# Splitting two more key chunks and sharing every low half with GpSimd

## The chip, the cores and the metric

The kernel runs on one core of one Trainium2 chip. The metric is the device time of one launch in microseconds; a change is measured against the kernel before on the same chip.

## The reference

Cross attention of 128 queries over 12,544 context rows, then a linear attention and a gated feed-forward on the 128 rows. The change touches only the scores of the cross attention (`Sim`, whose rows go through a softmax):

```python
Sim = (encoder_hc @ w1)[:, :, None] + (decoder_hq @ w2)[:, None, :] \
    + jnp.einsum('bid,bjd->bij', encoder_hc * w3, decoder_hq) + b_sim[0]
A = jax.nn.softmax(Sim, axis=2)
hq_hat = jnp.einsum('bij,bjd->bid', A, decoder_hq)
...
x = x + _L0_xattn_ref(_layernorm(x, axis=-1), ctx_1024, ...)
x = x + _L0_attn_ref(_layernorm(x, axis=-1), ...)
x = x + _L0_ffn_ref(_layernorm(x, axis=-1), ...)
```

## The kernel before, in words

The context is read twice from HBM: first transposed, as 25 key chunks of 512 columns (the last has 256), then as 25 chunks of rows. Each chunk is 512 KB and lands in one of ten slots of `raw`. SyncE issues all the loads in order (L396 to L413); a load into a slot waits (`wait_for_slot`, L380) until the slot's old content has been used: for a native chunk its matmuls, for a split chunk VectorE's low half, for a shared chunk GpSimd's part as well.

In the **key stage** TensorE computes `scores(k)` for k = 0 to 24 (L912). A **native** chunk (`NATIVE`, L35) multiplies fp32 keys from `raw` by the fp32 queries (L925). A **split** chunk is first taken apart into `pair`: ScalarE copies the keys rounded to the matmul format fp32r (the high half, `keys_high`, L488), VectorE subtracts that from the keys (the low half, `keys_low`, L698). TensorE then makes three passes over it, each of two matmuls: queries high by keys high (L940), queries low by keys high (L944), queries high by keys low (L954). `pair` has five buffers, used in turn. For a **shared** chunk (`SHARED`, L36) VectorE makes only the first 576 of the 1024 columns of the low half, and GpSimd the last 448 (L449 to L456). GpSimd's part of chunk k waits for VectorE's low half of the split chunk before k and for ScalarE's high half of k; TensorE waits for it only before the last matmul of the third pass (L953).

VectorE's queue in this stage is written out by hand (L758 to L762): for each pair of chunks (2e, 2e+1) the low halves of chunks 2e+2 and 2e+3 (none for native ones), then `running_max(e)` (L721), which takes the scores of chunks 2e and 2e+1 out of PSUM, negates them and carries the running maximum on. TensorE may be six chunks ahead of it (L919). ScalarE's queue (L557 to L579) holds the high halves in order, with work on the weights between them behind chunks 8, 12, 13, 16, 17, 18, 20 and 22.

In the **row stage** the scores become probabilities (ScalarE, L507), TensorE turns them (L968), ScalarE and VectorE split the turned block (L520, L728), and TensorE multiplies it by the rows (L997, L999). The rows are split too: ScalarE copies the first 512 columns of the high half (L488), GpSimd casts the other 512 (L463), VectorE makes the low half of all 1024 (L698). `row_use(k)` counts the split chunks through both stages, so the number of split key chunks moves the buffers that the row stage uses. The first two row chunks are multiplied in fp32 (L979). A short **tail** behind it does the rest of the layer.

Of the kernel before, what the change touches and what calls it, by code (L numbers as in the profile page):

```python
# [31 lines left out]
LATE = CHUNKS - 2  # L32
EARLY = 2
EPS = 1e-5
NATIVE = (0, 4, 8, 16, 24)  # L35
SHARED = (10, 12, 14, 18, 20, 22)  # L36
POOL_COLUMNS = 448
W_BEHIND = (12, 18)

# [22 lines left out]
def build(nc, x, keys_in, keys_last_in, rows_in, rows_last_in, weights_in, vec_in, bias_in, const_in, out):  # L62
# [6 lines left out]
    def width_of(k):  # L69
        return tiles_of(k) * P  # L70

    def is_native(k):

        return k in NATIVE

# [24 lines left out]
    with ExitStack() as stack:  # L100
# [271 lines left out]
        def keys_part(buf, k, a):  # L372
            return buf[:, a * width_of(k):(a + 1) * width_of(k)]
# [5 lines left out]
        def _(sp):  # L379
            def wait_for_slot(item):  # L380
# [10 lines left out]
                else:  # L391
                    sp.wait_ge(low_done, split_before[before] + 1)
                    if before in SHARED:
                        sp.wait_ge(pool_low_done, SHARED.index(before) + 1)

# [23 lines left out]
        def _(pool):  # L419
# [16 lines left out]
            for a in range(DH):  # L436
# [11 lines left out]
                                    ALU.mult, ALU.add).then_inc(mu_left_done, 1)  # L448
            for n, k in enumerate(SHARED):  # L449
                use = split_before[k]  # L450
# [236 lines left out]
        def _(dve):  # L687
# [8 lines left out]
            def take_low(item, use, columns):  # L696
                dve.wait_ge(high_done, use + 1)
                nc.vector.tensor_tensor(out=pair[:, use % PAIR_BUFS, 1, 0:columns], in0=raw[:, slot(item), 0:columns],  # L698
                                        in1=pair[:, use % PAIR_BUFS, 0, 0:columns].bitcast(F32), op=ALU.subtract)\
                    .then_inc(low_done, 1)  # L700

            def keys_low(k):

                take_low(k, split_before[k], ITEM - POOL_COLUMNS if k in SHARED else width_of(k) * DH)

# [200 lines left out]
        def _(pe):  # L906
# [5 lines left out]
            def scores(k):  # L912
# [36 lines left out]
                for a in range(DH):  # L949
                    if use == 0 and a > 0:  # L950
                        pe.wait_ge(low_done, 1)
                    if k in SHARED and a == DH - 1:
                        pe.wait_ge(pool_low_done, SHARED.index(k) + 1)  # L953
                    last = nc.tensor.matmul(out_ps, q_high[:, a, :], keys_part(low, k, a), start=False,  # L954
# [273 lines left out]
```

## Time and profile before

| | us |
|---|---|
| median of 3 runs (lowest to highest) | 112.36 (111.89 to 112.43) |
| the profiled execution | 112.1 |
| its span, first to last instruction | 110.3 |
| TensorE busy | 105.1 (95%) |
| VectorE busy | 93.1 (84%) |
| ScalarE busy | 82.4 (75%) |
| GpSimd busy | 29.3 (27%) |

Times within the trace are counted from the start of the span. The granted TensorE clock was 1.0 over the whole span. PE is TensorE's matmuls and PEld its weight loads, DVE is VectorE, ACT ScalarE, POOL GpSimd, SPq the queue of SyncE. The recorded length of an instruction overlaps the next one by some 0.1 us on VectorE and more on TensorE, so that paces are read from start to start.

### The profile page before, as it was taken

How to read it: one execution, taken by the hardware profiler on the slowest of the kernel's cores; microseconds unless marked ns; L12 is line 12 of the kernel's file. 1: busy time of each engine (PE TensorE's matmuls, PEld its weight loads, DVE VectorE, ACT ScalarE, POOL GpSimd, SP SyncE). 2: the span in 40 equal slices, each digit the busy share in tenths (PEclk: the TensorE clock that was granted, in tenths of full speed). 3: DMA queues.
4: the chain of work that ended last, by engine and by line, in shares of the span. 5: the costliest groups of instructions: out<-in, count | busy, mean ns of one | idle time of the engine just before them, and what ended most of it. 6: DMA issues, size and time to landing. Idle time of an engine off the chain costs nothing.

```text
span 110.3 us, 1855 instructions
## 1 busy us (share of the span) xinstructions
PE 105.1 (95%) x582; PEld 86.4 (78%) x583; DVE 93.1 (84%) x152; ACT 82.4 (75%) x171; POOL 29.3 (27%) x47
## 2 busy tenths in 40 slices
PE   5999999999999999999999999999999998998890
PEld 2368768588858888899899999989898997887680
DVE  1478999999998998999999999999999847674352
ACT  5067668899979989999999899988976725903450
POOL 2239200444043314233242424286330000200100
PEclk9999999999999999999999999999999999999999
DMA  2999999999999999999999999960000000000001
GB/s 72 367 406 423 416 422 422 416 422 422 409 420 417 418 415 423 417 420 442 442 389 423 415 422 425 406 260 0 3 0 0 0 6 0 0 0 0 6 3 48
DMA packets 8220, 29.82 MB, mean 270 GB/s; under 512 B 1042, under 2 KB 1298, under 8 KB 8082
## 3 DMA queue, kind: packets, MB, share of 16 engines
q1 hardware_dynamic: 8064, 29.69, 66.3%
q8 instruction: 5, 0.08, 0.3%
q14 instruction: 5, 0.04, 0.1%
q10 hardware_dynamic: 146, 0.01, 0.1%
HBM read 29.57 MB, written 0.13 MB: 269 GB/s over the span
## 4 chain that ended last, share of the span: by engine, by line
PE 94%; DVE 1%; issue 1%; ACT 1%; DVEq 0%; ACTq 0%
PE mixed_ps L997 18%; PE scores_ps L968 10%; PE mixed_ps L999 9%; PE scores_ps L940 8%; PE scores_ps L944 8%; PE scores_ps L954 8%; PE scores_ps L925 7%; PE scores_ps L910 4%; PE scores_ps L979 3%; PE scores_ps L1090 2%; PE mixed_ps L1142 2%; PE side_ps L1016 1%; PE scores_ps L1155 1%; PE side_ps L1133 1%; PE scores_ps L1016 1%; PE scores_ps L1125 1%
## 5 line engine op out<-in xcount | busy, mean ns | idle before, releaser
L698 DVE TENSOR_TENSOR pair<-raw,pair 128x1024 fp32r<-128x1024 f32 (+2 forms) x42 | 49.0, 1183 | 1.3 <-ACT pair L488 1.0
L488 ACT ACTIVATE pair<-raw 128x512 fp32r<-128x512 f32 (+1 forms) x42 | 34.5, 820 | 3.8 <-DMA raw<-keys_dram 3.4
L997 PE MATMUL mixed_ps<-pair,turned_high 128*128 128x512 f32 x84 | 32.3, 418 | 0.0
L999 PE MATMUL mixed_ps<-pair,turned_low 128*128 128x256 f32 x84 | 23.6, 281 | 0.0
L463 POOL CAST pair<-raw 128x512 fp32r<-128x512 f32 x22 | 13.6, 619 | 27.3 <-DVE pair L698 23.1
L997 PEld LDWEIGHTS mixed_ps<-pair,turned_high 128*128 128x128 f32 x84 | 15.8, 188 | 2.8
L520 ACT ACTIVATE turned_high<-scores_ps 128x512 fp32r<-128x512 f32 (+1 forms) x23 | 13.4, 584 | 4.0 <-PE scores_ps L968 4.0
L721 DVE TENSOR_SCALAR_CACHE_REDUCE neg_scores<-scores_ps,neg_max 128x1024 f32<-128x1024 f32 (+1 forms) x13 | 15.8, 1216 | 0.2
L999 PEld LDWEIGHTS mixed_ps<-pair,turned_low 128*128 128x128 f32 x84 | 16.0, 190 | 0.0
L728 DVE TENSOR_TENSOR turned_low<-scores_ps,turned_high 128x512 fp32r<-128x512 f32 (+1 forms) x23 | 15.3, 667 | 0.2 <-ACT turned_high L520 0.2
L968 PE MATMUL scores_ps<-ident,neg_scores 128*128 128x128 f32 x98 | 14.6, 272 | 0.0
L940 PE MATMUL scores_ps<-pair,q_high 128*128 128x512 f32 x40 | 14.1, 434 | 0.0
L507 ACT ACTIVATE neg_scores<-neg_scores,neg_max 128x1024 f32<-128x1024 f32 (+2 forms) x14 | 13.7, 977 | 0.0
L968 PEld LDWEIGHTS scores_ps<-ident,neg_scores 128*128 128x128 f32 x98 | 11.7, 140 | 1.4
L944 PE MATMUL scores_ps<-pair,q_low 128*128 128x512 f32 x40 | 12.5, 393 | 0.0
L954 PE MATMUL scores_ps<-pair,q_high 128*128 128x512 f32 x40 | 12.4, 391 | 0.0
L454 POOL TENSOR_TENSOR pair<-raw,pair 128x448 fp32r<-128x448 f32 x6 | 6.9, 1154 | 20.5 <-DVE pair L698 20.5
L940 PEld LDWEIGHTS scores_ps<-pair,q_high 128*128 128x128 f32 x40 | 7.5, 188 | 3.1 <-issue 1.9
L954 PEld LDWEIGHTS scores_ps<-pair,q_high 128*128 128x128 f32 x40 | 7.5, 188 | 1.7
L944 PEld LDWEIGHTS scores_ps<-pair,q_low 128*128 128x128 f32 x40 | 7.5, 188 | 1.6
L925 PE MATMUL scores_ps<-raw,q_t 128*128 128x512 f32 (+1 forms) x20 | 8.6, 553 | 0.0
L430 POOL TENSOR_TENSOR ln_rstd<-ln_var,minus_half 128x1 f32<-128x1 f32 x3 | 1.7, 555 | 21.8 <-DVE ln_var L842 12.7
(189 smaller groups left out, 130.6 us busy)
## 6 DMA issues: line engine op xcount, KB each, us to landing
raw<-keys_dram SPq DMA_DIRECT2D x24, 512.0 KB, 10.0
raw<-rows_dram SPq DMA_DIRECT2D x24, 512.0 KB, 9.2
w<-weights_dram SPq DMA_DIRECT2D x1, 1792.0 KB, 9.9
w<-weights_dram SPq DMA_DIRECT2D x2, 512.0 KB, 10.4
const<-const_dram SPq DMA_DIRECT2D x1, 832.0 KB, 11.5
raw<-keys_last_dram SPq DMA_DIRECT2D x1, 256.0 KB, 10.2
raw<-rows_last_dram SPq DMA_DIRECT2D x1, 256.0 KB, 6.8
x_sb<-x_dram SPq DMA_DIRECT2D x1, 128.0 KB, 2.2
```

The source lines that it names most:

```text
L488: nc.scalar.activation(pair[:, use % PAIR_BUFS, 0, 0:columns], raw[:, slot(item), 0:columns], ACT.Copy)\
L507: nc.scalar.activation(neg_scores[:, first:last], neg_scores[:, first:last], ACT.Exp, bias=neg_max[:, EVICTIONS:EVICTIONS + 1], scale=-1.0 ...
L698: nc.vector.tensor_tensor(out=pair[:, use % PAIR_BUFS, 1, 0:columns], in0=raw[:, slot(item), 0:columns], in1=pair[:, use % PAIR_BUFS, 0, 0 ...
L721: nc.vector.tensor_scalar(neg_scores[:, first_col:last_col], scores_ps[:, first // 2 % 3, scores_at:scores_at + last_col - first_col], -1. ...
L728: nc.vector.tensor_tensor(out=turned_low[:, k % TURNED_BUFS, 0:width_of(k)], in0=probs_turned_ps[k % TURNED_BUFS][:, 0:width_of(k)], in1=t ...
L925: last = nc.tensor.matmul(out_ps, q_t[:, a, :], keys_part(raw[:, slot(k), :], k, a), start=(a == 0), stop=(a == DH - 1))
L940: nc.tensor.matmul(out_ps, q_high[:, a, :], keys_part(high, k, a), start=(a == 0), stop=False)
L944: nc.tensor.matmul(out_ps, q_low[:, a, :], keys_part(high, k, a), start=False, stop=False)
L954: last = nc.tensor.matmul(out_ps, q_high[:, a, :], keys_part(low, k, a), start=False, stop=(a == DH - 1))
L968: last = nc.tensor.transpose(probs_turned_ps[k % TURNED_BUFS][:, t * P:(t + 1) * P], neg_scores[:, col:col + P], ident[:, :])
L997: nc.tensor.matmul(mixed_ps[:, :].rearrange("p (h d) -> p h d", h=2), probs_high, both[:, :, t * D:(t + 1) * D], start=(k == EARLY and t = ...
L999: last = nc.tensor.matmul(mixed_ps[:, 0:D], probs_low, rows_tile(high, t), start=False, stop=(k == LATE - 1 and end))
```

## The change

Two constants. Chunks 8 and 16 are no longer native; the shared chunks are all from 6 to 23 instead of six even ones.

```diff
-NATIVE = (0, 4, 8, 16, 24)
-SHARED = (10, 12, 14, 18, 20, 22)
+NATIVE = (0, 4, 24)
+SHARED = tuple(range(6, 24))
 POOL_COLUMNS = 448
```

So `scores(8)` and `scores(16)` take the split branch, ScalarE and VectorE get `keys_high` and `keys_low` of both, VectorE's low halves of chunks 6 to 23 have 576 columns, and GpSimd's loop over `SHARED` has 18 parts of 448 columns, each with its wait for the low half of the chunk before (`low_done`), in SyncE's `wait_for_slot`, and in TensorE's third pass.

## Rows read from the trace of the kernel before

**Rows 1.** The page: busy time of the engines, the chain that ended last, key loads.

```profile
PE 105.1 (95%) x582; PEld 86.4 (78%) x583; DVE 93.1 (84%) x152; ACT 82.4 (75%) x171; POOL 29.3 (27%) x47
...
PE 94%; DVE 1%; issue 1%; ACT 1%; DVEq 0%; ACTq 0%
...
raw<-keys_dram SPq DMA_DIRECT2D x24, 512.0 KB, 10.0
```

**Rows 2.** The chain in order of time: start us, length us, what.

```profile
19.22 1.72 PE scores_ps L925 x4
20.93 0.45 PE scores_ps L940 x2
21.39 0.46 PE scores_ps L944 x2
21.85 0.46 PE scores_ps L954 x2
...
30.54 1.72 PE scores_ps L925 x4
...
35.92 0.46 PE scores_ps L954 x2
...
40.05 0.47 PE scores_ps L954 x2
...
41.89 0.44 PE scores_ps L968 x4
42.33 0.87 PE scores_ps L925 x4
```

**Rows 3.** Busy time by engine from 22.77 to 25.78 us: PE, PEld, DVE, ACT, POOL.

```profile
22.77:25.78 3.01, 3.01 (x14) 2.46 (x14) 3.01 (x6) 2.80 (x6) 1.16 (x1) 1.00 1.02 416
```

**Rows 4.** Timeline of VectorE, key stage: start us, length us (of all merged), instruction.

```profile
13.94 1.28 DVE L721 TENSOR_SCALAR_CACHE_REDUCE neg_scores<-scores_ps,neg_max 128x1024 f32<-128x1024 f32 x1
...
22.77 1.28 DVE L721 TENSOR_SCALAR_CACHE_REDUCE neg_scores<-scores_ps,neg_max 128x1024 f32<-128x1024 f32 x1
23.97 1.89 DVE L698 TENSOR_TENSOR pair<-raw,pair 128x576 fp32r<-128x576 f32 x2
24.64 1.22 DVE L698 TENSOR_TENSOR pair<-raw,pair 128x1024 fp32r<-128x1024 f32 x1
25.78 1.28 DVE L721 TENSOR_SCALAR_CACHE_REDUCE neg_scores<-scores_ps,neg_max 128x1024 f32<-128x1024 f32 x1
...
38.92 1.88 DVE L698 TENSOR_TENSOR pair<-raw,pair 128x576 fp32r<-128x576 f32 x2
```

**Rows 5.** Timeline of GpSimd, the same stretch.

```profile
22.93 1.16 POOL L454 TENSOR_TENSOR pair<-raw,pair 128x448 fp32r<-128x448 f32 x1 [1.86 <-DVE pair L698]
```

**Rows 6.** Timelines of VectorE and GpSimd, 8.8 to 11.6 us.

```profile
9.18 2.36 DVE L698 TENSOR_TENSOR pair<-raw,pair 128x1024 fp32r<-128x1024 f32 x2 [0.50 <-ACT pair L488]
...
8.80 0.19 POOL L440 TENSOR_TENSOR b_kept<-b_c 128x2 f32<-128x2 f32 x1
8.95 0.20 POOL L442 TENSOR_TENSOR b_mean_sum<-b_mean 128x1 f32<-128x1 f32 x1
9.22 1.22 POOL L445 TENSOR_TENSOR mean_const<-b_mean_sum,ln_mv 128x1 f32<-128x1 f32 x1
10.41 1.18 POOL L447 TENSOR_SCALAR mu_left<-vec 128x4 f32<-128x4 f32 x1
```

**Rows 7.** The same at 44 to 46 us, and lengths of L698 (ns, min/median/max).

```profile
44.23 0.62 POOL L463 CAST pair<-raw 128x512 fp32r<-128x512 f32 x1 [0.62 <-DMA raw<-rows_dram]
...
44.24 2.81 DVE L698 TENSOR_TENSOR pair<-raw,pair 128x1024 fp32r<-128x1024 f32 x2
...
45.84 1.21 DVE L698 TENSOR_TENSOR pair<-raw,pair 128x1024 fp32r<-128x1024 f32 x1
...
L698 DVE TENSOR_TENSOR pair<-raw,pair x42: 675/1220/1681, 9.2 to 85.5; 128x1024 fp32r<-128x1024 f32 x35, 128x576 fp32r<-128x576 f32 x6, 128x512 fp32r<-128x512 f32 x1
```

**Rows 8.** The same in the row stage, one chunk.

```profile
66.37 0.62 POOL L463 CAST pair<-raw 128x512 fp32r<-128x512 f32 x1 [1.23 <-DVE pair L698]
...
66.73 1.32 DVE L698 TENSOR_TENSOR pair<-raw,pair 128x1024 fp32r<-128x1024 f32 x1
67.98 0.68 DVE L728 TENSOR_TENSOR turned_low<-scores_ps,turned_high 128x512 fp32r<-128x512 f32 x1
```

**Rows 9.** ScalarE: high halves, busy time from 26 to 32 us, who waited.

```profile
15.33 0.51 ACT L547 ACTIVATE x_c<-x_sb,x_neg_mean 128x256 f32<-128x256 f32 x1
16.70 1.06 ACT L488 ACTIVATE pair<-raw 128x1024 fp32r<-128x1024 f32 x1 [0.86 <-DMA raw<-keys_dram]
...
26.00:32.00 6.00, 6.00 (x25) 4.32 (x23) 6.00 (x8) 5.38 (x13) 1.81 (x2) 1.00 1.02 414
...
33.55 1.22 DVE L698 TENSOR_TENSOR pair<-raw,pair 128x1024 fp32r<-128x1024 f32 x1 [0.47 <-ACT pair L488]
```

## The prediction

> **What bounds the kernel now.** I read the page first. TensorE is busy for 95% of the span and is 94% of the chain that ended last [rows 1], so the first question for any edit is what it does to TensorE's queue. The chain in order of time [rows 2] gives the queue's true pace, without the overlap that the mean durations hold: a native key chunk (fp32 straight from raw) takes 1.72 us (chunk 8 at 19.22, chunk 16 at 30.54), a split chunk three passes of 0.46 us, 1.37 in all, and each piece begins where the one ahead ends. There is no gap in it from chunk 4 to the row stage, and behind the keys the chain goes on unbroken (probabilities turned at 41.89, the short chunk 24 at 42.33). So in the key stage TensorE is the bound, at 2.75 us for a pair of split chunks.
>
> Next come the engines that feed it, because a faster TensorE is worth only what they can follow. VectorE was busy in all of the 3.01 us of the pair from 22.77 to 25.78, and ScalarE in 2.80 of them [rows 3]. From start to start VectorE's pieces are [rows 4]: the maximum over a pair of chunks (L721) 1.20 us (22.77 to 23.97), a low half of 576 columns 0.67 (23.97 to 24.64), one of all 1024 columns 1.14 (24.64 to 25.78). That is 3.01 for a pair of which one chunk is shared with GpSimd, slower than TensorE's 2.75; VectorE lives off a lead that it won before, and by the end little is left. It starts low half 22 at 38.92 and ends it at 39.59, and TensorE's third pass over it starts at 40.05 [rows 2, 4]. So the key stage is close to having VectorE as its bound.
>
> GpSimd's part of a shared chunk (L454, 448 columns) takes 1.16 us. In the kernel before it is released by VectorE's low half of the odd chunk ahead, so it starts together with the maximum: 22.93 to 24.09, beside L721 from 22.77 to 23.97 [rows 4, 5]. The two never run low halves side by side, but for 0.1 us. After the change they must.
>
> **What a low half and a GpSimd instruction do to each other.** This is the row that decides the case. Two tiny GpSimd instructions on 2 columns and 1 column took 0.19 and 0.20 us at 8.80 and 8.95, when VectorE stood idle. The next, on 1 column, started at 9.22, 0.04 us behind a low half of 1024 columns (9.18), and took 1.22 us: it ended at 10.44, when that low half was over (10.32). The one at 10.41 took 1.18 beside the second low half [rows 6]. So a running low half (two SBUF inputs) holds GpSimd off to its end, and GpSimd then gets its turn ahead of the next one. The other way round: at 44.23 a GpSimd cast of 0.62 us started together with a low half at 44.24, and VectorE's next low half came only at 45.84, 1.60 later and not 1.14; the slowest of all low halves is 1681 ns [rows 7]. The cast cost VectorE 0.46 us, its whole length but for the last 0.16. At 66.73 a low half met the last 0.26 us of a cast (66.37 to 66.99) and took 1.25 from start to start, 0.11 more than 1.14 [rows 8]: again all but the last 0.15. The maximum reads PSUM, and it took 1.28 with GpSimd beside it as it did without [rows 4]. My reading is mutual exclusion between low halves and GpSimd's reads.
>
> The Trainium skill speaks against this change too (SBUF — State Buffer, "Who interferes with whom"): a VectorE instruction with two SBUF inputs and a GpSimd instruction that reads SBUF exclude each other for the whole instruction, the second waiting until the first ends. The rows agree on the block, but show it 0.15 us shorter than the whole; taken to the letter, the rule would put 0.14 us more on each of the eight waits below, some 1 us on the sum.
>
> **The change, part by part.** (1) Chunks 8 and 16 split: TensorE saves 2 x (1.72 - 1.37) = 0.69 us, if it is fed. (2) ScalarE gets two high halves of 1.06 us [rows 9]. The first fits into the 0.86 us in which it waited for data at 15.84 and the slack behind; the second falls in 26 to 32, where ScalarE has 0.62 us idle, so that later high halves come about 0.4 us later. Alone this is hidden: low half 19 waited 0.47 us for ScalarE at 33.55 [rows 9], shrinks by 0.47, and TensorE has its third pass over it at 35.92. I cost it at nothing; the price if the cover is gone is the 0.4. (3) VectorE: 12 low halves of the 18 chunks go from 1.14 or nothing to 0.67: ten shrink by 0.47 (4.7 us saved), two are new (1.34 spent), 3.4 us less work. (4) GpSimd goes from 6 to 18 parts, 18 x 1.16 = 21 us of work in the 28 us of these chunks (13.94 to 41.89). (5) The load into a slot now waits for GpSimd's part as well; the queue is some 10 us of transfers deep (10.0 us from issue to landing [rows 1]), so a release some us late costs nothing in the key stage, and rows are read far later. (6) The buffer numbers of the row stage move by two; no cost.
>
> Without exclusion VectorE would need 1.20 + 2 x 0.67 = 2.54 us a pair, under TensorE's 2.75: that is the good case. With it the pair runs like this. GpSimd's part of an odd chunk is released by the low half of the even one, finds VectorE in the odd low half, and starts when that ends, which is when the maximum starts. It takes 1.16. The part of the next even chunk, long released, follows at once, at +1.16, while the maximum ends at +1.20: VectorE's even low half comes 0.04 us too late and waits until GpSimd's read ends, 1.16 - 0.14 after its start, at +2.18. Then two low halves, 1.34. The period is 1.20 + 0.98 + 1.34 = 3.52 us. Were VectorE first at that point, GpSimd's part would slip in between the two low halves and the period would be the same.
>
> Where it starts: low halves 6 and 7 run 15.14 to 16.48 (the maximum ahead of them starts at 13.94 [rows 4]). GpSimd's part 7 then runs 16.48 to 17.64, its part 8 from 17.64, and VectorE's low half 8, due at about 17.9, gets in at 18.66 and ends at 19.33. Seven periods on, low half 22 ends at 19.33 + 7 x 3.52 = 43.97, where it now ends at 39.59. TensorE's third pass over 22 starts some 0.13 later, at 44.10 instead of 40.05: 4.05 us late. GpSimd's part 23 runs 44.64 to 45.80, which adds 0.14 before the last matmul of chunk 23. The 0.69 is inside this sum, since TensorE now waits. The row stage behind is TensorE's own and moves as a whole. Sum: +4.2 us. The profiled execution took 112.1 (span 110.3), so it would be 116.3; the median of the runs is 112.36, 0.26 above it, and I forecast 116.5.
>
> Bounds on the one unknown, how long a 448-column tensor_tensor of GpSimd holds VectorE off, which no row shows for more than 0.16 us: the cast held it for 0.46 of 0.62, 74%; at that share a part would hold it 0.86 and not 1.02, the period is 3.36 and the sum 3.1. At 1.16 in full and 0.05 us between, the period is 3.7 and the sum 5.4. I take 1.02, since both casts show a fixed tail of about 0.15.
>
> **The rivals.** *No exclusion between these two instructions* (GpSimd's part reads two inputs by turns and may leave room). Place: VectorE's even low half. Price: none, and the gain of part (1) stands, 112.36 - 0.69 = 111.7. It decides from where VectorE's wait is below 2.75 - 2.54 = 0.21 us a pair. For it: at 22.93 and five more times such a part overlaps the low half by 0.1 us without harm. Against it: the tail of a cast does none either, and the body of one does; and low halves would in any case hold GpSimd off, as 9.22 shows.
> *Partial exclusion:* half the wait, 0.49 a pair. Low half 8 ends at 18.84, the period is 3.03, and low half 22 ends at 18.84 + 7 x 3.03 = 40.05; TensorE's third pass starts at 40.18 and not 40.05, and with the 0.14 of part 23 that is 0.3 us, 112.6.
> *ScalarE sets the pace* after the exclusion turns out harmless: the 0.4 us of part (2) eats most of the 0.69, giving about 112.1, within the measurement.
> *The change does nothing* is excluded: both constants enter the loops directly.
>
> **How the numbers follow.** Full exclusion, +3.1 to +5.4: 0.80. No exclusion with the gain: 0.11. Partial exclusion or a late ScalarE: 0.09, of which two thirds lie within 0.5% (0.56 us, about what a measurement of this kernel can tell from no change). So faster 0.11, same 0.06, slower 0.83. The range runs from 114.0, below the low bound of 115.5 since the hold may be softer than a cast's, to 118.0, the high bound; it leaves out the cases near 112.
>
> **What would show it.** In the profile after: low halves (L698) of 576 columns in two kinds, about 0.75 us and about 1.7, the long ones on even chunks; L454 of odd chunks at 1.6 to 1.7 us, as their wait is inside the record; maxima starting 3.5 us apart; TensorE idle before L954 for 0.8 us a pair; the turn at 41.89 moved to about 46. If instead all L698 stay at 0.75 and the maxima stand 2.75 apart, the exclusion was wrong and the time is 111.7. If the hold is real but the time moved little, look for a period near 3.0. If ScalarE is late, VectorE's idle time before L698 names L488.

## The result and the profile after

The changed kernel takes 115.88 us (median of 6 runs, 115.45 to 116.51); the kernel before, run beside it, 112.18 (111.89 to 112.43). The ratio is 1.0335, with a 95% interval from 1.03 to 1.037: slower by 3.7 us. The profiled execution took 116.03 us, its span is 114.3. Ratios leave out the launches in a slower state of the chip and medians do not, so that below a ratio can be a little smaller than the medians make it. Beside the experiments the kernel before had medians of 112.21 to 112.43.

From the page of the kernel after, the lines that answer to [rows 1], and what the DMA engines moved in 40 equal slices of the span:

```profile
PE 107.0 (94%) x586; PEld 85.8 (75%) x587; DVE 96.6 (85%) x154; ACT 84.3 (74%) x173; POOL 44.6 (39%) x59
...
GB/s 98 351 412 417 423 422 416 423 422 417 417 417 415 414 419 359 298 310 270 361 402 386 420 416 422 422 384 46 3 0 0 6 0 0 0 0 3 6 0 46
...
PE 57%; DVE 18%; issue 11%; DMA 7%; SPq 2%; ACT 2%; DVEq 0%; ACTq 0%
```

The busy shares hardly tell that anything happened: TensorE stands at 94% and was at 95%. The chain does. TensorE has fallen from 94% of it to 57%, and VectorE, which had 1%, has 18%, with 11% of "issue", time for which the profile names no cause. In order of time, two pairs of the key stage:

```profile
26.36 0.75 DVE pair L698
27.11 1.20 DVE neg_scores L721 x2
28.32 0.06 DVE pair L698
28.38 1.41 issue
29.79 0.74 DVE pair L698
30.53 1.21 DVE neg_scores L721 x2
...
43.60 0.73 PE scores_ps L954 x2
...
45.79 0.44 PE scores_ps L968 x4
```

The chain runs through VectorE with a period of 3.42 us: maximum 1.20, the even low half with what it waits (0.06 and 1.41 of "issue"), the odd one 0.74. It gets back to TensorE at 43.60, at the third pass over chunk 22, and the turn that was at 41.89 [rows 2] is at 45.79, 3.90 us later. The span grew by 4.0. So all of the loss but 0.1 us was made in the key stage.

The timeline of VectorE in that stretch, and that of GpSimd:

```profile
28.24 2.29 DVE L698 TENSOR_TENSOR pair<-raw,pair 128x576 fp32r<-128x576 f32 x2
30.45 1.27 DVE L721 TENSOR_SCALAR_CACHE_REDUCE neg_scores<-scores_ps,neg_max 128x1024 f32<-128x1024 f32 x1
31.66 0.08 DVE L721 DVE_READ_ACCUMULATOR neg_scores<-scores_ps,neg_max 128x1 f32 x1
31.66 2.29 DVE L698 TENSOR_TENSOR pair<-raw,pair 128x576 fp32r<-128x576 f32 x2
33.88 1.27 DVE L721 TENSOR_SCALAR_CACHE_REDUCE neg_scores<-scores_ps,neg_max 128x1024 f32<-128x1024 f32 x1
```

```profile
29.94 2.72 POOL L454 TENSOR_TENSOR pair<-raw,pair 128x448 fp32r<-128x448 f32 x2 [0.70 <-DVE pair L698]
33.36 2.73 POOL L454 TENSOR_TENSOR pair<-raw,pair 128x448 fp32r<-128x448 f32 x2 [0.70 <-DVE pair L698]
```

Two low halves of 576 columns take 2.21 us from start to start (28.24 to 30.45), where two unhindered ones take 2 x 0.67 = 1.34 [rows 4]: VectorE waits 0.87 us a pair. GpSimd's two parts follow each other without a gap, the first already waiting while VectorE makes the odd low half. One blocked low half by itself, the low halves of 576 columns as a group (us busy, mean ns) after and before, and GpSimd's parts (ns: min/median/max) show the blocked ones of both engines:

```profile
21.40 1.62 DVE L698 TENSOR_TENSOR pair<-raw,pair 128x576 fp32r<-128x576 f32 x1
...
L698 DVE TENSOR_TENSOR pair<-raw,pair 128x576 fp32r<-128x576 f32 x18 | 19.8, 1139 | 0.0
...
L698 DVE TENSOR_TENSOR pair<-raw,pair 128x576 fp32r<-128x576 f32 x6 | 4.5, 754 | 0.0
...
L454 POOL TENSOR_TENSOR pair<-raw,pair x18: 1143/1380/1617, 14.4 to 43.6; 128x448 fp32r<-128x448 f32 x18
```

The waits within these records are in no list of waits, since no semaphore ends them; VectorE's idle time before L698 is 1.1 us in all. What the list of waits does name is the victim:

```profile
PEld scores_ps L954 <- DVE pair L698: 5.1, 7, 0.7
...
PE scores_ps L954 <- DVE pair L698: 2.1, 7, 0.3
PEld scores_ps L954 <- POOL pair L454: 1.8, 8, 0.2
```

### The profile page after: what moved, and what is told of

Same layout as the page of the kernel before. It is cut to its first block, busy times and chain, and to the rows that moved or that the text cites. A ratio compares the mean times of both kernels' runs of the same rounds, so it can differ in the third digit from the quotient of the medians.

```text
span 114.3 us, 1905 instructions
## 1 busy us (share of the span) xinstructions
PE 107.0 (94%) x586; PEld 85.8 (75%) x587; DVE 96.6 (85%) x154; ACT 84.3 (74%) x173; POOL 44.6 (39%) x59
## 4 chain that ended last, share of the span: by engine, by line
PE 57%; DVE 18%; issue 11%; DMA 7%; SPq 2%; ACT 2%; DVEq 0%; ACTq 0%
PE mixed_ps L997 17%; DVE neg_scores L721 10%; PE scores_ps L968 9%; PE mixed_ps L999 9%; DVE pair L698 7%; DMA raw<-keys_dram 7%; PE scores_ps L979 3%; SPq L401 2%; PE scores_ps L1090 2%; PE mixed_ps L1142 1%; PE side_ps L1016 1%; PE scores_ps L954 1%; PE scores_ps L1155 1%; PE side_ps L1133 1%; PE scores_ps L1016 1%
## 5 line engine op out<-in xcount | busy, mean ns | idle before, releaser
L698 DVE TENSOR_TENSOR pair<-raw,pair 128x1024 fp32r<-128x1024 f32 (+2 forms) x44 | 52.5, 1213 | 1.1 <-ACT pair L488 1.1
L488 ACT ACTIVATE pair<-raw 128x512 fp32r<-128x512 f32 (+1 forms) x44 | 36.2, 830 | 2.8 <-DMA raw<-keys_dram 2.5
L454 POOL TENSOR_TENSOR pair<-raw,pair 128x448 fp32r<-128x448 f32 x18 | 24.6, 1380 | 11.3 <-DVE pair L698 11.3
L954 PE MATMUL scores_ps<-pair,q_high 128*128 128x512 f32 x44 | 15.0, 422 | 2.1 <-DVE pair L698 2.1
L940 PE MATMUL scores_ps<-pair,q_high 128*128 128x512 f32 x44 | 14.6, 412 | 0.0
L944 PE MATMUL scores_ps<-pair,q_low 128*128 128x512 f32 x44 | 13.7, 393 | 0.0
L954 PEld LDWEIGHTS scores_ps<-pair,q_high 128*128 128x128 f32 x44 | 7.7, 188 | 7.9 <-DVE pair L698 5.1
L940 PEld LDWEIGHTS scores_ps<-pair,q_high 128*128 128x128 f32 x44 | 8.2, 188 | 2.5 <-issue 0.7
L944 PEld LDWEIGHTS scores_ps<-pair,q_low 128*128 128x128 f32 x44 | 8.3, 188 | 1.9
L910 PE MATMUL scores_ps<-idle 128*128 128x512 bf16 x12 | 5.0, 568 | 1.2 <-DVE idle L733 1.2
## 6 DMA issues: line engine op xcount, KB each, us to landing
const<-const_dram SPq DMA_DIRECT2D x1, 832.0 KB, 11.6
```

What stands on the lines that cost most here:

```text
L454: nc.gpsimd.tensor_tensor(out=pair[:, use % PAIR_BUFS, 1, shared], in0=raw[:, slot(k), shared], in1=pair[:, use % PAIR_BUFS, 0, shared].bi ...
L488: nc.scalar.activation(pair[:, use % PAIR_BUFS, 0, 0:columns], raw[:, slot(item), 0:columns], ACT.Copy)\
L940: nc.tensor.matmul(out_ps, q_high[:, a, :], keys_part(high, k, a), start=(a == 0), stop=False)
L944: nc.tensor.matmul(out_ps, q_low[:, a, :], keys_part(high, k, a), start=False, stop=False)
```

## The experiments

Two theories stood against each other. **Exclusion:** a low half with two SBUF inputs and a GpSimd instruction that reads SBUF cannot run together; what two of GpSimd's parts stick out beyond the maximum, VectorE waits. **The chain of semaphores:** GpSimd is merely slow, or its waits and VectorE's are linked in a ring of 3.42 us, and no resource is shared. In the profiles the key stage is measured from the start of chunk 4 to the turn before chunk 24, since the first keys land some tenths earlier or later from one execution to the next, which moves everything behind them: 13.21 to 41.73 us in the timeline of the kernel before, 28.52 us; 13.05 to 45.63 after, 32.58, so +4.06.

### VectorE's second operand from PSUM

```diff
-in1=pair[:, use % PAIR_BUFS, 0, 0:columns].bitcast(F32)
+in1=side_ps[:, 0:1].to_broadcast([P, columns])    # the 576-column low halves only
```

> The changed kernel, but VectorE's 576-column low halves read their second operand from PSUM (one column, spread) and not from SBUF, so the low halves of the shared chunks are not the keys' own. The order of the work, the waits, the sizes and GpSimd's parts stay. Theory (a low half with two SBUF inputs and GpSimd's SBUF reads exclude each other): both exclusions go, L698 of 576 columns is 0.75 to 0.8 us throughout, L454 1.15 throughout, the maxima stand 2.75 us apart (TensorE's pace), and the time is 0.4 to 0.7 us below the kernel before, 111.5 to 111.8. Rival (the 3.42 us come from the chain of semaphores and from GpSimd's own length, or from any overlap with it): L454 and the maxima stay as after, about 115.9.

Measured: 112.53 us, ratio 1.0029 (0.9989 to 1.0069). Its groups, and a stretch of VectorE's timeline (the edit moved line 698 to 701, and 721 to 724):

```profile
L454 POOL TENSOR_TENSOR pair<-raw,pair 128x448 fp32r<-128x448 f32 x18 | 20.6, 1162 | 8.2 <-DVE pair L701 5.2 <-ACT pair L488 3.0
...
L701 DVE TENSOR_TENSOR pair<-raw,side_ps 128x576 fp32r<-128x576 f32 x18 | 12.9, 749 | 1.5 <-ACT pair L488 1.5
```

```profile
22.33 1.29 DVE L724 TENSOR_SCALAR_CACHE_REDUCE neg_scores<-scores_ps,neg_max 128x1024 f32<-128x1024 f32 x1
23.54 0.08 DVE L724 DVE_READ_ACCUMULATOR neg_scores<-scores_ps,neg_max 128x1 f32 x1
23.54 1.41 DVE L701 TENSOR_TENSOR pair<-raw,side_ps 128x576 fp32r<-128x576 f32 x2
25.08 1.28 DVE L724 TENSOR_SCALAR_CACHE_REDUCE neg_scores<-scores_ps,neg_max 128x1024 f32<-128x1024 f32 x1
```

The same queues, waits and columns, and only one operand of VectorE's low halves differs: it stands in PSUM, and it is one column spread over 576. All 18 parts of GpSimd are 1132 to 1175 ns, all 18 low halves near 749, and the maxima stand 2.75 us apart, TensorE's pace, but for two places where VectorE waited for a high half of ScalarE (0.38 us at 30.16, 1.10 at 33.88); no third pass of TensorE waited in the stage. The key stage is 27.82 us (13.54 to 41.36), 0.70 below the kernel before. The rival of the semaphore chain is out: it is the second SBUF input. (A single spread column in SBUF was not tried, so the place is not quite parted from the form; for the place speaks that GpSimd's part did not lengthen the maximum either, which reads PSUM: 1.27 to 1.28 us.) The median came out 0.7 to 1 us above what I expected, and cannot be told from the kernel before; the profiled execution (111.58) has the gain in its key stage and in its span, 109.8 against 110.3.

### GpSimd's part only writes

The `...` stand for what is left out, here and below; a semaphore, not shown, orders the two memsets.

```diff
-nc.gpsimd.tensor_tensor(out=pair[..., 1, shared], in0=raw[...], in1=pair[..., 0, shared], op=ALU.subtract)
+nc.gpsimd.memset(filler[:, :], 0.0)                              # 640 columns, unused
+nc.gpsimd.memset(pair[..., 1, shared].bitcast(F32), 0.0)         # 448 columns
```

> The changed kernel, GpSimd's part being two memsets that only write (640 columns of an unused tile, then its 448 columns of the low half, filled with zeros), so those columns are not the keys' own. Theory (it is GpSimd's reads that exclude a low half): the memsets take as long beside a low half as alone, L698 of 576 columns stays at 0.75, maxima 2.75 apart: 111.5 to 111.9. Rival (any access of GpSimd to SBUF excludes a low half): even low halves wait for the memsets, and time rises with them, over 113.

Measured: 112.62 us, ratio 1.0 (0.9959 to 1.0041). Its groups (L698 is L701 here):

```profile
L701 DVE TENSOR_TENSOR pair<-raw,pair 128x576 fp32r<-128x576 f32 x18 | 13.1, 755 | 2.7 <-ACT pair L491 2.7
L458 POOL MEMSET filler<- 128x640 f32 x18 | 11.4, 635 | 14.3 <-DVE pair L701 9.8 <-ACT pair L491 4.4
L459 POOL MEMSET pair<- 128x448 f32 x18 | 8.5, 474 | 0.0
```

GpSimd is busy for 1.11 us a part, nearly as long as before (1.15), and in its turn beside low halves with both inputs in SBUF: neither waits for the other. So the write side is free, and the exclusion is one of reads. Of the time I expected too much: it is that of the kernel before and not 0.5 to 0.9 less, and the maxima do not stand 2.75 us apart. Most stand 2.54 apart, the 1.20 + 2 x 0.67 that VectorE needs when nothing holds it off, and three stand 3.16 to 3.72 apart, since VectorE waited 2.7 us in three places of the stage for ScalarE's high halves. TensorE waited by it for a first pass (0.25 us, at 34.98) and for a third (0.45 us, at 37.56); the key stage is 28.65 us.

### GpSimd's part is a copy

```diff
-nc.gpsimd.tensor_tensor(out=pair[..., 1, shared], in0=raw[...], in1=pair[..., 0, shared], op=ALU.subtract)
+nc.gpsimd.tensor_copy(out=pair[..., 1, shared], in_=raw[...])
```

> The changed kernel, GpSimd's parts being copies of 448 columns (one SBUF input) and not differences (two), so that part of the low half is not the keys' own. Number of parts, waits and VectorE's work stay. Theory: the parts fall to 0.54 us (a cast of 512 takes 0.62), two of them fit beside a maximum, L698 of 576 stays at 0.75, maxima 2.75 apart: 0.3 to 0.7 below the kernel before, 111.5 to 111.9. Rival (the count of switches between the engines is what costs, not how long GpSimd reads): near after, 115 or more.

Measured: 112.23 us, ratio 0.9978 (0.9942 to 1.0014), above the 111.5 to 111.9 that I had given; the key stage 28.26 us, 0.26 below the kernel before. Its groups (L698 is L697 here):

```profile
L454 POOL CAST pair<-raw 128x448 fp32r<-128x448 f32 x18 | 14.3, 803 | 14.5 <-DVE pair L697 8.6 <-ACT pair L487 5.7
L697 DVE TENSOR_TENSOR pair<-raw,pair 128x576 fp32r<-128x576 f32 x18 | 13.1, 754 | 2.1 <-ACT pair L487 2.0
```

The low halves are 754 ns, so VectorE never waits for GpSimd; the copies are 803 ns on average (556 to 1084), as those that are released beside a low half wait for its end within their record. As many switches between the engines as after, but shorter reads, and the loss is gone. What is missing to the gain of 0.69 is again a third pass that waited once (0.46 us) behind a late ScalarE.

### How much GpSimd reads: 224 and 336 columns

```diff
-POOL_COLUMNS = 448
+POOL_COLUMNS = 224    # the other: 336
```

> The changed kernel with GpSimd's part cut from 448 to 224 columns in every chunk from 6 to 23, VectorE's low half 800 columns. Theory (VectorE waits for what GpSimd's reads stick out beyond the maximum): two parts of some 0.67 us, the first started at the end of the odd low half, are nearly over when the 1.20 us of the maximum are, so VectorE waits 0.15 us at most and a pair costs 1.20 + 2 x 0.90 = 3.0 to 3.15 us. Fewer columns on GpSimd are faster: 0.2 to 1.3 us over the kernel before, 112.4 to 113.5, against 115.9 with 448. Rival (what counts is how much work VectorE hands over): slower than after, above 116.

> The changed kernel with 336 columns for GpSimd. Theory (VectorE waits for what two parts stick out beyond the maximum of 1.20 us): a part is 0.91 us, the second one's reads end 1.60 us after the start of the maximum, VectorE waits 0.40 and a low half of 688 columns is 0.79: the period is 1.20 + 0.40 + 1.57 = 3.17 us, between 3.01 (224 columns) and 3.42 (448), and the time 113.8 to 114.6. Rival (a step and no slope, once GpSimd's parts no longer fit): near 3.4 and 115.5 or more.

Measured: 224 columns 113.08 us, ratio 1.0051 (1.0012 to 1.0089); 336 columns 114.15 us, ratio 1.0152 (1.0086 to 1.0218). VectorE's timelines, first 224, then 336:

```profile
23.18 1.28 DVE L721 TENSOR_SCALAR_CACHE_REDUCE neg_scores<-scores_ps,neg_max 128x1024 f32<-128x1024 f32 x1
24.38 0.09 DVE L721 DVE_READ_ACCUMULATOR neg_scores<-scores_ps,neg_max 128x1 f32 x1
24.38 1.89 DVE L698 TENSOR_TENSOR pair<-raw,pair 128x800 fp32r<-128x800 f32 x2
26.19 1.28 DVE L721 TENSOR_SCALAR_CACHE_REDUCE neg_scores<-scores_ps,neg_max 128x1024 f32<-128x1024 f32 x1
```

```profile
23.40 1.27 DVE L721 TENSOR_SCALAR_CACHE_REDUCE neg_scores<-scores_ps,neg_max 128x1024 f32<-128x1024 f32 x1
24.60 0.08 DVE L721 DVE_READ_ACCUMULATOR neg_scores<-scores_ps,neg_max 128x1 f32 x1
24.60 2.04 DVE L698 TENSOR_TENSOR pair<-raw,pair 128x688 fp32r<-128x688 f32 x2
26.57 1.27 DVE L721 TENSOR_SCALAR_CACHE_REDUCE neg_scores<-scores_ps,neg_max 128x1024 f32<-128x1024 f32 x1
```

The periods are 3.01, 3.17 (as worked out) and, with 448, 3.42 us. VectorE's own work falls with every column it hands over, from 3.0 to 2.54 us a pair, and the pair gets longer all the same: the wait grows from nothing over 0.4 to 0.87. Handing over less is faster, down to 224 columns; with none at all (the next run) it is slower again.

### No GpSimd at all

```diff
-SHARED = tuple(range(6, 24))
+SHARED = ()
```

> The changed kernel with no shared chunk: VectorE makes all low halves of 1024 columns alone. Theory: a pair costs VectorE 1.20 + 2 x 1.14 = 3.48 us against 3.42 with GpSimd, so sharing both chunks of a pair buys nearly nothing: maxima 3.48 apart, 4.0 to 4.6 us over the kernel before, 116.2 to 116.8. Rival (GpSimd's help is real, and the 3.42 has another cause that VectorE alone would have too): much slower than after, since VectorE then has 2 x 0.47 more a pair: a period near 4.3, over 120.

Measured: 117.4 us, ratio 1.0449 (1.0393 to 1.0505), somewhat over the range I gave. In its timeline of VectorE:

```profile
28.03 1.28 DVE L721 TENSOR_SCALAR_CACHE_REDUCE neg_scores<-scores_ps,neg_max 128x1024 f32<-128x1024 f32 x1
...
31.51 1.28 DVE L721 TENSOR_SCALAR_CACHE_REDUCE neg_scores<-scores_ps,neg_max 128x1024 f32<-128x1024 f32 x1
```

The period is 3.48 us, which is just 1.20 + 2 x 1.14. So from chunk 8 on the parts, 24.6 us of GpSimd's records in all, buy 0.06 us a pair: 0.94 saved on the low halves, 0.87 given back as waiting. The one pair that gains more is the first, low halves 6 and 7, where no second part holds VectorE off: 1.39 us (15.39 to 16.78 after) against 2.27 (15.34 to 17.61 here). The key stage is 33.56 us, 0.98 above after.

### The two halves of the change alone, and GpSimd beside the maximum only

Even parts, against the changed kernel:

```diff
-SHARED = tuple(range(6, 24))
+SHARED = tuple(range(6, 24, 2))
```

Sharing only, against the kernel before:

```diff
-SHARED = (10, 12, 14, 18, 20, 22)
+SHARED = tuple(k for k in range(6, 24) if k not in NATIVE)
```

> The changed kernel with GpSimd's parts on even chunks only (6, 8, ... 22), 448 columns each. Every part then runs beside a maximum. Theory: period 3.01 as in the kernel before, both L698 kinds unblocked (0.75 and 1.22), L454 1.15; VectorE falls 0.26 us a pair behind TensorE and the time is 0.1 to 0.5 us over the kernel before: 112.3 to 112.7. So the split of chunks 8 and 16 alone costs next to nothing, and the odd parts cost 3 us. Rival (the cost lies in the two split chunks): stays above 114.

> The kernel before with every split chunk from 6 to 23 shared, chunks 8 and 16 native: the other half of the change alone. Theory: period 3.42 where both chunks of a pair are split, but the pairs with chunks 8 and 16 have one low half less, and TensorE gives 0.34 us there: 0.4 to 1.2 us over the kernel before, 112.6 to 113.4, so the two halves of the change are not additive. Rival (sharing costs the whole 3.7 us by itself): 115 or more.

Measured: even parts 113.11 us, ratio 1.0062 (1.0023 to 1.01); sharing only 113.69 us, ratio 1.0113 (1.0029 to 1.0198). Both times are above the ranges I had given (112.3 to 112.7 and 112.6 to 113.4). Even parts have unblocked records of both engines (L698 of 576 columns 756 ns, L454 1163) and a period of 3.01; their key stage is 29.39 us, 0.87 longer than that of the kernel before. VectorE, 0.26 us a pair slower than TensorE, has used up its lead by 25.55, and from there on six third passes wait for it. From VectorE's timeline with sharing only:

```profile
28.62 1.27 DVE L721 TENSOR_SCALAR_CACHE_REDUCE neg_scores<-scores_ps,neg_max 128x1024 f32<-128x1024 f32 x1
...
30.49 1.27 DVE L721 TENSOR_SCALAR_CACHE_REDUCE neg_scores<-scores_ps,neg_max 128x1024 f32<-128x1024 f32 x1
...
33.65 0.76 DVE L698 TENSOR_TENSOR pair<-raw,pair 128x576 fp32r<-128x576 f32 x1 [1.20 <-ACT pair L488]
```

Sharing only has the period of 3.4 us where both chunks of a pair are shared, but the pairs with a native chunk are short (the maxima of 28.62 and 30.49 stand 1.87 us apart), and VectorE wins back a lead there twice. A fully shared pair puts it 0.67 us behind TensorE (3.42 against 2.75), a pair with a native chunk brings it 1.22 forward (1.87 against 1.72 + 1.37). The native chunks were that lead. Each half alone costs 0.87 and 1.34 us in the key stage; together they cost 4.06, since what the one uses up the other would have needed. Not all of the 1.34 is exclusion, though: the second lead was lost at 33.65, where VectorE waited 1.20 us for a high half of ScalarE, which had itself waited 1.12 us for a key load at 30.20. What that wait is worth is not separated.

### Two attempts at a faster kernel

Both are the kernel before with these constants, the first called split 8, the second odd 512:

```diff
-NATIVE = (0, 4, 8, 16, 24)
-SHARED = (10, 12, 14, 18, 20, 22)
+NATIVE = (0, 4, 16, 24)
+SHARED = (6, 8, 10, 12, 14, 18, 20, 22)
```

```diff
-NATIVE = (0, 4, 8, 16, 24)
-SHARED = (10, 12, 14, 18, 20, 22)
-POOL_COLUMNS = 448
+NATIVE = (0, 4, 16, 24)
+SHARED = tuple(range(7, 24, 2))
+POOL_COLUMNS = 512
```

> The kernel before with chunk 8 alone split and shared, and chunk 6 shared too, so that all parts are on even chunks and beside a maximum: (6, 8, 10, 12, 14, 18, 20, 22). Theory: TensorE saves 0.34 us on chunk 8; VectorE has 0.67 more for low half 8 and 0.47 less for 6, which its lead at that place takes; chunk 16 stays native and renews the lead. Expected 0.35 us below the kernel before at best, 111.8, within what can be told apart. Rival (the lead does not last, as in the kernel with even parts and both split): 112.5 to 113.

> The kernel before with chunk 8 split, chunk 16 native, and GpSimd's parts on the odd chunks (7, 9, ... 23) with 512 columns. A part of an odd chunk is released while VectorE makes the odd low half and begins exactly when the maximum does, so 512 columns (some 1.2 us) fit beside it. Theory: no low half waits for GpSimd, L454 is 1.6 to 1.7 us with its own wait, the period is 1.20 + 1.14 + 0.60 = 2.94 us against 3.01, and over eight pairs VectorE is 0.5 us less late than with chunk 8 split and even parts of 448: the time comes back to that of the kernel before, 112.0 to 112.6, or a little under. Rival (a part of 512 columns sticks out beyond the maximum): low half 10 and its followers wait and the time is above 113.

Measured: split 8 112.95 us, ratio 1.0055 (1.0022 to 1.0088); odd 512 113.25 us, ratio 1.0046 (1.0004 to 1.0088). The trace of the latter is of a launch of 590.95 us, and nothing is read from it; its time is above the 112.0 to 112.6 that I had given, and why stays open. Split 8 went the way of its rival: its waits show three third passes that came late by VectorE (0.38 us at 27.89, 0.45 at 36.79, 0.40 at 39.80), its maxima stand 3.01 apart where both chunks are split, and the key stage is 0.46 longer. Even one more split chunk is more than VectorE can follow. Of the versions with all the work in them none beat the kernel before.

## Why the prediction was right

**The bound and who follows it.** TensorE was the bound by a margin of some tenths over VectorE, as read from [rows 2, 4]. The gain of part (1), 0.69 us, is real: with VectorE's operand in PSUM the key stage is 0.70 us shorter. But that kernel does not compute the low halves, and no version that does had the gain.

**Exclusion.** Read from two tiny GpSimd instructions and two casts [rows 6 to 8], it held for the pair of instructions that no row had shown side by side: the place of one operand takes it away, writes do not cause it, and its price follows the columns.

**The period** was to be 1.20 + 0.98 + 1.34 = 3.52 us and is 3.42. The term that was off is the wait, 0.87 and not 0.98, and the step behind it is where the second part starts. I let the part of the odd chunk take its full 1.16 us, counted from the end of the low half that held it off. It takes some 0.1 less: in the trace the maximum starts at 20.20, with the end of the odd low half, and GpSimd's next part at 21.26:

```profile
21.26 1.14 POOL L454 TENSOR_TENSOR pair<-raw,pair 128x448 fp32r<-128x448 f32 x1
```

My reading is that a part that waits within its record has its beginning behind it when the low half ends; no row shows what it does in that time. The rest, reads that end some 0.14 us before the record does, was right: 21.26 + 1.14 - 0.14 = 22.26, and the low half of 0.67 that follows is over at 22.93. So the Trainium skill's rule (SBUF — State Buffer, "Who interferes with whom"), by which the block lasts for the whole instruction, would have given a wait longer still, by some 0.14 us; these traces do not bear that out to the letter. Its other sentence there, that a GpSimd instruction which only writes does not contend with two SBUF inputs, agrees with the memsets (755 ns for L698 beside them).

**The sum.** +4.2 us was forecast for the profiled execution: 4.05 at the third pass over chunk 22 and 0.14 for GpSimd's part 23. The pass began at 43.60 and not 44.10: seven periods of 3.42 give 0.7 less than seven of 3.52, and low half 8 ended at 19.53 and not 19.33, as VectorE's start lay 0.25 us later in this execution (the maximum of 13.94 in [rows 4] is at 14.19), low halves 6 and 7 took 0.05 more, and the first wait was 0.1 shorter too. That makes 3.55. The missing 0.27 lies in the pass itself, which has 0.73 us in the chain after and had 0.47. Most of that is my own mixing of two starts. The chain counts a pass that did not wait from the end of the pass ahead (40.05), and one that waited from its own first record. Matmul records overlap, and in TensorE's timeline the pass over chunk 22 started earlier, first before, then after:

```profile
39.88 0.63 PE L954 MATMUL scores_ps<-pair,q_high 128*128 128x512 f32 x2
...
43.60 0.73 PE L954 MATMUL scores_ps<-pair,q_high 128*128 128x512 f32 x2 [0.30 <-DVE pair L698]
```

So the pass was 3.72 us late, not 3.55, and having waited cost it 0.10 more. Part 23 cost 0.08 (L954 at 45.25, 0.54 us, in the chain). 3.72 + 0.10 + 0.08 = 3.90, where the turn is. That the forecast came within 0.3 us of it owes something to luck: the wait was put 0.1 us too long on each of eight pairs, and the late pass was counted 0.17 + 0.10 us too short and VectorE's start 0.3 too early. The rest of the kernel moved as a whole, 4.0 at the end of the span. Against the median of the runs it is 3.7. The bounds were summed over seven pairs only: the wait before low half 8 belongs to them as well, which makes them 2.9 and 5.6 and not 3.1 and 5.4. The measured change lies inside either.

**What was costed at nothing** stayed so. ScalarE's two high halves: VectorE waits 1.1 us in all for L488 after and 1.0 before. Without exclusion ScalarE is next in line: with the copy and with the memsets a third pass waited once, 0.45 us, behind it, and there my rival of a late ScalarE was the right one. The loads: the DMA engines fall to 270 to 360 GB/s in slices 16 to 20, as slots are released later (SyncE's queue waits 17.4 us for GpSimd's parts and waited 3.6), and TensorE's path shows no wait for rows.

**What I had not seen** is how the native chunks enter. I took them for 0.34 us of TensorE each. They also spare VectorE a low half, 1.14 or 0.67 us in which it regains its lead; I take that to be the main reason why the two halves of the change do not add up.

## What to carry to other kernels

Before work goes to GpSimd, look not at its idle share but at which VectorE instructions it would run beside: in these traces it was free beside one that reads PSUM, and beside one with two SBUF inputs its reads and VectorE's followed each other. So count how much of GpSimd's reading fits beside VectorE's instructions that read PSUM, and hand over no more (here one part of 448 columns per maximum of 1.20 us, which the kernel before had). Such a wait lies inside the records. It shows up as "issue" in the chain and as a group of one shape with two lengths, and in no list of waits. A short GpSimd instruction that takes six times its usual length beside VectorE's (1.22 us and 0.20) was enough to find it before the change was made.

## What the runs showed of the hardware

A GpSimd difference of two operands took 0.67 us for 224 columns and 1.15 for 448, some 2.1 ns a column, twice as much as VectorE needs (0.67 for 576 from start to start); a memset 0.47 us for 448 columns. The exclusion goes both ways and seems to alternate: in no row read here did one engine get two turns while the other one waited; who wins when both ask at once was not tried. New to me was that the blocked one seems partly prepared: 0.1 us of a GpSimd part's 1.15 is not paid again behind the block (the next part starts 1.06 us after it).
